# A cross-attention, self-attention and Sinkhorn-mixing layer on one core: the last product blocks tile by tile, three Sinkhorn chains with other work between their steps, and tile 3 in two halves

## What is computed

```python
x = x + _L0_attn_ref(_layernorm(x), Wq, Wk, Wv, Wo)          # ends with out @ Wo.T
z = _layernorm(x)
# third block, on z; n = 4 streams of C = 256 columns
z_norm = z * rsqrt(mean(z * z) + RMS_EPS)
H_res_logits = (z_norm @ W_res.T).reshape(B, T, n, n) + H_res_base
H_pre, H_post = softmax(z_norm @ W_pre.T + base), softmax(z_norm @ W_post.T + base)
H_res = sinkhorn_log(H_res_logits)     # 50 iterations of row and column scaling, tau 0.1
H_res = (1.0 - g) * I + g * H_res      # g = sigmoid(gate)
y = einsum('btnc,btn->btc', streams, H_pre) @ W_branch
out = x + einsum('btij,btjc->btic', H_res, streams) + einsum('btc,btn->btnc', y, H_post)
```

## Time and profile before

| | us |
|---|---|
| median of 3 runs | 1110.79 (1109.37 to 1111.04) |
| profiled execution, its time | 1110.1 |
| profiled execution, its span | 1108.3 |
| TensorE busy | 1068.6 (96%) |
| VectorE busy | 815.5 (74%) |
| ScalarE busy | 479.4 (43%) |

### The profile page before, as it was taken

How to read it: one execution, slowest core, us unless ns; L and a number is a source line. 1 busy time by engine, 2 the same in 40 slices (tenths; PEclk the granted TensorE clock), 3 DMA queues, 4 the chain that set the end, 5 groups by cost and what they waited for, 6 DMA issues and landing times.

```text
span 1108.3 us, 17664 instructions
## 1 busy us (share of the span) xinstructions
PE 1068.6 (96%) x6336; PEld 894.6 (81%) x6336; DVE 815.5 (74%) x1919; ACT 479.4 (43%) x1022; POOL 194.8 (18%) x190
## 2 busy tenths in 40 slices
PE   6999999999999999999999999999999999999668
PEld 4888888788888888888888888888888878887546
DVE  6887668667667869766678877667537788747998
ACT  4544434444444446544444465424213343431316
POOL 2000000223223233333233230000001032230000
PEclk9999999999999999999999999999999999999789
DMA  9975775244543333344445312799935514000002
GB/s 239 174 198 126 162 161 141 54 113 107 109 109 80 72 76 72 71 97 95 111 97 109 76 36 55 152 219 243 207 65 107 87 33 66 3 14 1 1 1 77
DMA packets 184685, 111.27 MB, mean 100 GB/s; under 512 B 108056, under 2 KB 174616, under 8 KB 184624
## 3 DMA queue, kind: packets, MB, share of 16 engines
q1 hardware_dynamic: 182368, 109.37, 45.6%
q10 hardware_dynamic: 2256, 1.11, 0.5%
HBM read 90.98 MB, written 18.94 MB: 99 GB/s over the span
## 4 chain that ended last, share of the span: by engine, by line
PE 88%; DVE 9%; DMA 1%; ACT 1%; issue 0%; SPq 0%; DVEq 0%
PE ps L624 32%; PE ps L524 15%; PE ps L591 14%; PE ps L958 9%; PE ps L508 4%; PE ps L652 4%; PE ps L635 4%; PE ps L735 1%; DVE small L2088 1%; DVE small L2080 1%; DVE small L2092 1%; DVE small L2084 1%; DVE small L2076 1%; DVE small L2072 1%; DMA raw<-in_L_xattn_q_proj_w 1%; PE ps L868 1%
## 5 line engine op out<-in xcount | busy, mean ns | idle before, releaser
L624 PE MATMUL ps<-wt,act 128*128 128x512 f32 x1536 | 381.0, 394 | 0.0
L624 PEld LDWEIGHTS ps<-wt,act 128*128 128x128 f32 x1536 | 278.0, 188 | 51.8 <-issue 0.4
L524 PE MATMUL ps<-wt,act 128*128 128x512 f32 x768 | 178.7, 393 | 1.5 <-ACT act L1083 0.8
L524 PEld LDWEIGHTS ps<-wt,act 128*128 128x128 f32 x768 | 144.5, 189 | 33.4 <-ACT wt L1088 3.0
L591 PE MATMUL ps<-act,wt 128*128 128x512 f32 x672 | 153.7, 390 | 0.0
L1088 ACT ACTIVATE wt<-raw 128x512 fp32r<-128x512 f32 x192 | 106.6, 625 | 95.5 <-PE ps L524 52.3
L591 PEld LDWEIGHTS ps<-act,wt 128*128 128x128 f32 x672 | 125.8, 188 | 26.0
L1534 DVE STREAM_TRANSPOSE raw<-raw 128x1024 f32<-128x1024 f32 x92 | 107.9, 1216 | 21.7 <-DMA raw<-in_L_xattn_o_proj_w 21.7
L958 PE MATMUL ps<-wt,act 128*128 128x512 f32 x480 | 121.4, 400 | 0.0
L1542 DVE TENSOR_TENSOR wt<-raw,wt 128x512 fp32r<-128x512 f32 x172 | 107.4, 682 | 17.3 <-ACT wt L1088 17.2
L2248 POOL TENSOR_TENSOR small<-small 128x4 f32<-128x4 f32 (+2 forms) x64 | 69.0, 1079 | 245.3 <-DVE small L1556 199.6
(11 more groups left out here) (168 smaller groups left out, 1257.1 us busy)
## 6 DMA issues: line engine op xcount, KB each, us to landing
xr<-in_ctx SPq DMA_DIRECT2D x64, 256.0 KB, 4.8
raw<-in_L_xattn_o_proj_w SPq DMA_DIRECT2D x32, 512.0 KB, 14.1
raw<-in_L_xattn_q_proj_w SPq DMA_DIRECT2D x28, 512.0 KB, 9.5
xr<-q_rows SPq DMA_DIRECT2D x16, 512.0 KB, 4.2
ot_hi<-spare SPq DMA_DIRECT2D x64, 128.0 KB, 2.0
act<-ot_hi SPq DMA_DIRECT2D x32, 256.0 KB, 9.3
q_rows<-G SPq DMA_DIRECT2D x28, 256.0 KB, 2.9
raw<-in_L_xattn_k_proj_w SPq DMA_DIRECT2D x8, 512.0 KB, 7.0
```

What stands on the lines that cost most here:

```text
L524: mm = pe.matmul(banks[t], lhs(p == 2, c, t), wt[:, n_slot, int(p == 1), c, :], start=(acc_from and q == 0), stop=(acc_to and q == 3 * NC ...
L624: mm = pe.matmul(bank, src[int(p == 2)][:, c, kt * P:(kt + 1) * P], wt[:, slot, int(p == 1), c, :], start=(q == 0), stop=(q == 3 * NC - 1))
```

## The change

- `LAST` and `TURNED`: the last four blocks come as (2,0), (2,1), (3,0), (3,1) instead of (2,0), (3,0), (2,1), (3,1). The accumulator bank follows the block's number, not the tile. Turns and logits of tile 2 move into block 14; the first turn and half of the logits of tile 3 into block 15.
- Three chains: chain 0 is tiles 0 and 1, chain 1 is tile 2, chain 2 is tile 3. `iterate` gets an argument `beside`, called between its steps. The add and statistics of blocks (2,0), (2,1), (3,0) and the whole start of chain 1 are issued there, one piece between two steps of chain 0.
- Chain 0 iterates alone nine times, then beside chain 1 five times. Then chain 2 is started with nothing beside it. After it, chains 1 and 2 are taken together as one of 32 columns, tile 2 being 5 iterations ahead, beside chain 0 for 35 iterations. When chain 0 is finished they are parted again: 8 iterations together, then tile 2 is finished while tile 3 does one, then tile 3 does 4 alone and is finished.
- The folding is at iteration 21 of tile 3 (26 of tile 2) instead of 25.
- Tile 3 is mixed in two halves: i = 0 and 1 by VectorE (8 instructions instead of 16), i = 2 and 3 by ScalarE and TensorE (8 diagonals, 2 products with the identity, 8 products, 2 copies), behind tile 2's. ScalarE's `diagonals(3)` stand between the copies of tile 2's third and fourth quarter. In ScalarE's stream `exp_chain(1)` now stands ahead of `copy_rows(3, 0)`.
- SyncE stores in eight transfers instead of seven.

The diff, cut to its core:

```diff
-LAST = ((0, 0), (1, 0), (0, 1), (1, 1), (2, 0), (3, 0), (2, 1), (3, 1))
+LAST = ((0, 0), (1, 0), (0, 1), (1, 1), (2, 0), (2, 1), (3, 0), (3, 1))
...
-                                             (2, 2, 3, mix_out, 6), (3, 0, 2, out_ready, 1), (3, 2, 4, out_ready, 2),
-                                             (2, 3, 4, mix_out, 7)):
+                                             (2, 2, 3, mix_out, 6), (2, 3, 4, mix_out, 7), (3, 2, 3, mix_out, 8),
+                                             (3, 0, 2, out_ready, 1), (3, 3, 4, mix_out, 9)):
...
+                    elif b == 14:
+                        turn_rows(2, 1)
                     elif b == 15:
-                        logits(3, 0, 4)
+                        turn_rows(3, 0)
...
                     elif b == 14:
-                        turn_rows(3, 0)
+                        logits(2)
                     elif b == 15:
-                        turn_rows(2, 1)
+                        logits(3, 0, 4)
...
-                    if b == 15:
-                        logits(2)
...
-            mix(2)
+            mix(2, 0, 2)
+            pe.wait_ge(mix_out, 4)
+            for i in (2, 3):
+                pe.matmul(mix_bank(3, i), ident[:], xr[:, 3, i * CW:(i + 1) * CW], start=True, stop=False)
+            mix(2, 2, 4)
+            mix(3, 2, 4)
...
             exp_chain(0)
             copy_rows(2, 0)
-            copy_rows(3, 0)
             copy_rows(2, 1)
             normalise_out(2)
+            exp_chain(1)
+            copy_rows(3, 0)
             copy_rows(3, 1)
-            exp_chain(1)
+            exp_chain(2)
             normalise_out(3)
...
             diagonals(2)
             mixed(2, 0)
-            mixed_quarter(2)
-            mixed_quarter(3)
+            mixed_quarter(2, 2)
+            diagonals(3)
+            mixed_quarter(2, 3)
+            mixed_quarter(3, 2)
+            mixed_quarter(3, 3)
...
-            tiles = [(0, 2), (2, 2)]
+            tiles = [(0, 2), (2, 1), (3, 1)]
...
+            def iterate(chains, beside=None):
...
+                if beside:
+                    beside(0)
                 for c in chains:
                     sum_rows(c, Kx if c in fold else tk)
+                if beside:
+                    beside(1)
...
+            def add_first(t):
+                def beside(k):
+                    if k == 1:
+                        add_rows(t, 0)
+                    elif k == 3:
+                        first_stats3(t)
+                return beside
+
+            def add_second(t):
+                def beside(k):
+                    if k == 1:
+                        add_rows(t, 1)
+                    elif k == 3:
+                        late_stats3(t)
+                    elif k == 5:
+                        end_stats3(t)
+                return beside
+
+            def begin_first(c):
+                def beside(k):
+                    if k == 0:
+                        centre_logits(c + 1)
+                    elif k == 1:
+                        scale_logits(c + 1)
+                    elif k == 2:
+                        sharpen(c)
+                    elif k == 3:
+                        peak_rows(c)
+                    elif k == 4:
+                        centre_rows(c)
+                    else:
+                        peak_cols(c)
+                return beside
+
+            def begin_second(c):
+                def beside(k):
+                    if k == 0:
+                        first_rows(c)
+                    elif k == 1:
+                        centre_cols(c)
+                    elif k == 2:
+                        answered(c, 2)
+                        scale_rows(c)
+                    elif k == 3:
+                        sum_cols(c)
+                    elif k == 4:
+                        invert_cols(c)
+                return beside
...
+            begin(0)
+            iterate((0,))
+            iterate((0,), add_first(2))
+            for _ in range(2):
                 iterate((0,))
-            add_last(3, 0)
-            for _ in range(LEAD[1]):
+            iterate((0,), add_second(2))
+            for _ in range(2):
                 iterate((0,))
...
+            iterate((0,), begin_first(1))
+            iterate((0,), begin_second(1))
+            iterate((0, 1), add_first(3))
+            for _ in range(3):
+                iterate((0, 1))
             add_last(3, 1)
...
+            iterate((0, 1))
+            centre_logits(3)
+            scale_logits(3)
+            sharpen(2)
+            peak_rows(2)
+            centre_rows(2)
+            peak_cols(2)
+            first_rows(2)
+            centre_cols(2)
+            branch_peaks()
+            answered(2, 2)
+            scale_rows(2)
+            sum_cols(2)
+            invert_cols(2)
+
+            ahead = iterated[1] - iterated[2]
+            iterated[1] = iterated[2]
+            tiles[1], ua[1], ub[1] = (2, 2), uv[:, 8:16], uv[:, 24:32]
+            stepped(2)
             for k in range(ITERS - iterated[0]):
                 iterate((0, 1))
...
+            tiles[1], ua[1], ub[1] = (2, 1), uv[:, 8:12], uv[:, 24:28]
+            iterated[2] = iterated[1] + 1
+            iterated[1] = iterated[2] + ahead
             stepped(1)
             for _ in range(ITERS - iterated[1]):
                 iterate((1, 2))
...
+            finish_cols(1)
+            scale_cols(2)
+            finish_gate(1)
+            sum_rows(2, tk)
+            finish_diagonal(1)
+            invert_rows(2)
+            scale_rows(2)
+            sum_cols(2)
+            invert_cols(2)
+            iterated[2] += 1
+            for _ in range(ITERS - iterated[2]):
+                iterate((2,))
+            finish_cols(2)
+            finish_gate(2)
+            finish_diagonal(2)
...
-            mix(((3, 0), (3, 1)))
+            mix(((3, 0),))
```

More of the change, by code:

```diff
@@ L939, in base, with mix, tile_products @@
                 mm.then_inc(base_done, 1)
-            def mix(t):
-                for i in range(NSTR):
+            def mix(t, i0=0, i1=NSTR):
+                for i in range(i0, i1):
                     for j in range(NSTR):
-                        pe.wait_ge(d_res, 16 * t + 4 * i + j + 1)
+                        pe.wait_ge(d_res, 16 * t + 4 * i + j + 1 - (8 if t == 3 else 0))
                         mm = pe.matmul(mix_bank(t, i), dres[t % 2][:, 4 * i + j, :], z[:, t, j * CW:(j + 1) * CW],
-                                       start=False, stop=j == NSTR - 1 and (i % 2 == 1 or (t, i) == (2, 2)))
-                    if i % 2 == 1 or (t, i) == (2, 2):
+                                       start=False, stop=j == NSTR - 1 and (i % 2 == 1 or (t >= 2 and i == 2)))
+                    if i % 2 == 1 or (t >= 2 and i == 2):
                         mm.then_inc(mix_done, 1)
-            def tile_products(n, t, at_11, at_17, at_5=None):
+            def tile_products(n, t, at_11, at_17, at_5=None, bank=None):
                 for q in range(3 * NC):
@@ L1477, in diagonals @@
             def diagonals(t):
-                sc.wait_ge(h_ready, t // 2 + 1)
+                sc.wait_ge(h_ready, max(t, 1))
                 if t >= 2:
                     sc.wait_ge(mix_done, 2 * (t - 2) + 2)
-                for n in range(16):
+                for n in range(8 if t == 3 else 0, 16):
                     sc.activation(dres[t % 2][:, n, :], ident[:], ACT.Copy, scale=hres[:, 16 * t + n:16 * t + n + 1]
@@ L1964, in _, with add_rows @@
             turns = {1: (22, (0, 1, 2, 3)), 2: (23, (0, 1)), 4: (23, (2,)), 5: (23, (3,)), 8: (24, (0, 1)), 9: (24, (2, 3))}
+            def add_rows(t, half):
+                k = LAST.index((t, half))
+                v.wait_ge(acc_done, 77 + k)
+                y = xr[:, t, half * UW:(half + 1) * UW]
+                done(v.tensor_tensor(y, acc2[k % 2], y, ALU.add), acc_free)
             def add_last(t, half):
-                add_tile(77 + LAST.index((t, half)), t, half, acc2)
+                add_rows(t, half)
                 if half == 0:
@@ L2092, in invert_cols, with begin @@
                 step(c, v.reciprocal(ub[c], ub[c]))
-            def first_iteration3(c):
+            def begin(c):
+                sharpen(c)
[4 more added lines that the diff above has]
+                centre_cols(c)
                 answered(c, 2)
@@ L2102, in fold_outer @@
                 stepped(c)
-                rows = two(ua[c]).unsqueeze(3).broadcast_to([P, 2, NSTR, NSTR])
+                rows = two(ua[c]).unsqueeze(3).broadcast_to([P, tiles[c][1], NSTR, NSTR])
                 step(c, v.tensor_tensor(rows4(of(tk, c)), rows, over_i(ub[c]), ALU.mult))
@@ L2109, in fold_root @@
                 step(c, v.tensor_tensor(of(dst, c), of(tk, c), of(A, c), ALU.mult))
-            iterated = [1, 1]
-            def iterate(chains):
-                fold = [c for c in chains if iterated[c] == EPOCH]
+            iterated, folds = [1, 1, 1], [EPOCH, EPOCH - 4, EPOCH - 4]
+            def iterate(chains, beside=None):
```

(7 more changed lines are left out.)

109 lines of the change are left out of this document (52 added, 57 removed).

## The result

Over 22 runs each, the changed kernel took 1112.42 us in the median and the kernel before 1109.80 us; the ratio is 1.0018, 95% interval 1.0012 to 1.0024. The ratio is that of the means, without one run of each kernel that lies far out (6108.31 us before; 1549.15 us, at a low clock, changed); the medians alone stand as 1.0024. By the ratio the change is 2 us slower. That lies at the bound that the prediction drew for "no change" (0.2%), on the slow side, where it had placed its forecast of +1.4 us. The profiled execution of the changed kernel has a span of 1110.5 us, against 1108.3 us before.

The account below looks back on a forecast made before the run. TensorE's queue was taken to set the tail: last add +0.3 us, chain 0's end 2.5 us earlier, tail 3.97 us longer, together +1.4 us. On a median of 1110.8 us this gave 1112.2 us, range 1110.6 to 1115.0 us.

Parts of the forecast that it names:

- no change: Whole kernel: a measurement tells 0.2%, or 2.2 us, from no change; the forecast was placed within it.
- The bound: Tail: TensorE, already full while the chains still run, sets the end; tile 3's earlier chain gains nothing.
- the chain sets the end: Rival, tail: TensorE is through with tile 2 when tile 3's values come; 3.4 us less, 1107.4 us; chance 0.08.
- The product blocks: Last four product blocks: no stall at (2,1), TensorE stalls some 0.7 us at (3,0); last add +0.3 us.
- the blocks slip: Rival, product blocks: add or copy of (3,0) over 0.8 us later, everything moves, 1113.0 to 1115.0 us; chance 0.21.
- Start and iterations: Tile 3's start and joint loop: loop from 1028.8, 35 turns instead of 37, first diagonal 2.5 us earlier at 1079.85.
- steps beside a chain cost their full duration: Rival, joint iterations: extra steps delay chain 0 by 5 to 8 us, 1117 to 1120 us; chance 0.03.
- The tail: First diagonal to last copy: ten more TensorE products, 4.3 us; 3.97 us longer from an origin 2.54 us earlier.
- at full clock: TensorE in the tail: 7.16 of 7.20 and 7.00 of 7.00 us busy at granted clock 1.00, the 2.4 GHz level.
- The sum: Whole kernel: new span 1109.7 us against 1108.3; median 1110.8 + 1.4 = 1112.2 us.
- within 0.2%: Whole kernel: outcome "same", no difference a measurement can tell, up to 2.2 us; chance 0.68.

Follow-up runs that it names:

- e2: Changed kernel without the last four iterations of tile 3 (46 instead of 50); ratio to the kernel before 1.0015.
- e4: Changed kernel with tile 3 mixed wholly by VectorE, as before the change; ratio to the kernel before 0.9995.
- e6: Kernel before with only tile 3's mixing in two halves, chains and product order as before; ratio to the kernel before 1.0047.
- e3: Changed kernel with the start of tile 3's chain between steps of two joint iterations instead of alone; ratio to the kernel before 1.0004.
- e9: Changed kernel with two more idle products, late, at eight steps before chain 0's end; ratio to the kernel before 1.0005.
- e5: Changed kernel itself, unchanged, run again on a second chip; ratio to the kernel before 1.0021.
- e10: Kernel before with two more idle products, late, at eight steps before chain 0's end; ratio to the kernel before 1.0002.
- e1: Changed kernel with six instead of four idle products ahead of mix(0), nothing else; ratio to the kernel before 1.0013.

## Why the prediction was right, and where it was off

**The bound (right).** That the tail would hang on TensorE's queue and not on the chains is shown by e2 (four iterations less of tile 3, no gain), e4 (more work on VectorE, faster) and e6 (the halves alone, 5.2 us slower). The rival "the chain sets the end" is out.

**The product blocks (right).** The stall of TensorE at the turn of (3,0) was forecast at 0.7 us; it came at that place and put the block back by 0.3 us (0.57 us of idle weight loads). Turn (2,1) found its rows in time. The last add came 0.15 us later in relation to the earlier blocks (1022.13 - 1003.79 = 18.34 us behind the turn of (2,0), before 1022.62 - 1004.43 = 18.19 us), against +0.3 us forecast. The rival "the blocks slip" did not happen.

**Start and iterations (right).** From the last add to the first diagonal I had 1079.85 - 1022.9 = 56.95 us; it is 57.22 us. The start alone took 1028.33 - 1025.56 = 2.77 us. The rival "steps beside a chain cost their full duration" is out: a step of chain 0 and one of chain 1 go as a pair every 0.23 us (the iterations of the changed kernel between 1017.77 and 1021.70). It begins to hold from the third instruction on: 0.28 us a step in e3.

**The tail (mechanism right, one term missing).** I had 27.16 us from the first diagonal to the last copy; measured 28.56 us. With the clock at the 2.4 GHz level it is 27.04 us (e2, e9), so the count of products, the 0.4325 us for each, and the order of ScalarE's queue were right to 0.1 us. The step that failed is the one that carried "at full clock" from the earlier trace rows of the kernel before over to the changed one: mix(0) and mix(1) were costed by their 14.08 us at a clock of 1.00, and took 15.60 us. The idle products ahead of them keep their place in chain 0, but chain 0 now ends 2.5 us earlier behind the last add (57.22 instead of 59.77 us), while branch and base, TensorE's work before them, do not come earlier (base ends 47.4 us behind the last add, before 46.3). In the changed kernel the idle products begin 2.26 us behind base's last product, in the kernel before 5.81 us:

```profile
1071.75 5.37 PE L1049 MATMUL ps<-G,ident 128*128 128x512 f32 x8 [2.26 <-DVE small L2129]
```

```profile
1074.78 6.54 PE L1048 MATMUL ps<-G,ident 128*128 128x512 f32 x8 [5.81 <-DVE small L2092]
```

The clock was still up when they began, and fell 0.9 us later; in the kernel before it had fallen 1.0 us ahead of them. Of the changed kernel, then of the kernel before:

```profile
1071.75:1072.50 0.75, 0.75 (x2) 0.45 (x3) 0.75 (x8) 0.00 (x0) 0.00 (x0) 1.00 0.00 0
```

```profile
1074.00:1075.00 1.00, 0.22 (x1) 0.25 (x2) 1.00 (x10) 0.00 (x0) 0.00 (x0) 0.50 0.00 0
```

From their start to the first product of mix(0) it is 8.05 us in the changed kernel and 8.06 us before. As they took 5.37 instead of 6.54 us, the gap behind them grew to 2.69 us. Their duration does not hang on their start alone: in e4 they began 4.94 us behind base and took 5.37 us too. But the five profiles with the chains of the changed kernel and these four products (changed, e2, e4, e5, e9) have 5.10 to 5.64 us, and the three with the chains of the kernel before (before, e6, e10) 5.86 to 6.54 us. That the idle products could be left as they were is a term that the prediction put at nothing without naming it. The low clock in mix(0) and mix(1) cost 1.5 us in the profile; that the longer gap brought it on is supported, and not shown beyond doubt (e5, e9).

**The sum.** By the profiled executions the span grew by 2.2 us where I had 1.4. By the medians it grew by 2.6 us. That my 1112.2 us nevertheless lies 0.2 us from the measured 1112.42 is two errors that cancel: the base of three runs, 1110.79 us, was 1.0 us above the median of 22, and the step was 1.2 us too small. From the last add to the last copy the profile grew by 2.8 us (-2.55 for the chains, +5.37 for the tail) where I had 1.15 (-2.82 and +3.97). The chance of 0.68 for "within 0.2%" was given to an outcome that turned out at the edge of it.

## What to carry to other kernels

Before work is moved from one engine to another at the end of a kernel, add up the queue of the engine that receives it from the moment it starts, not from the moment the moved work is ready. Here TensorE was full for 15 us before that, and ten more products cost their whole 4 us, while the chain that was to be relieved had stopped mattering. Where idle products are to hold TensorE's clock, tie their end to the event that they bridge to (a late trigger): their own duration here was anything from 3.67 to 6.54 us for the same four products, by the clock that they found, and the gap behind them moved with it. And compare more than one profile before a clock level is put into a sum. Starting one chain alone cost the others 2.0 us here, and that shows in the time because the next stage hangs on them.

## What the runs showed of the hardware

TensorE's clock fell to the 1.2 GHz level in five of seven profiles in which it stood idle between 1.88 and 3.34 us after the idle products, and in none of five with 0.48 to 1.52 us. All five falls were in executions in which the clock had also been at 0.50 in `branch`; the two that were spared (gaps of 2.42 and 2.69 us) had not. The fall came between 0.3 us before the first product of mix(0) (changed kernel) and 0.8 us behind it (e1). Where it fell, the 64 rows of 128x256 took 15.6 to 15.8 us instead of 14.08 us, and the clock was back 3.1 us (changed kernel) to 4.2 us (e1) behind that first product. The Trainium skill (TensorE: Matmul & The Clock Gate, Part 1: The HAM clock gate (the "warmup" mystery)) says that the throttled state is the default, that activity releases it, and that the moment of release varies from run to run. These profiles agree on both; they show besides that the fall varies too, as a gap of 2.69 us was followed by it in two profiles (changed, e5) and not in a third (e4). I had not expected that idle products which run faster can do harm: six of them at 1.00 took 5.39 us (e1), four mostly at 0.50 took 5.37 us.
